# One large and one small output store, moved from ScalarE's DMA queue to the end of SyncE's, in an 8192 x 8192 adjacency product

## The chip, the cores and the metric

The kernel runs on one core of a Trainium2 chip. The time is the device time of one execution in microseconds (us). Three executions were timed; the median is 645.89 us. One more was profiled.

## The reference

```
keep   = (u >= 0.1)                       # u: 8192 x 64
x_drop = x * keep / 0.9                   # x: 8192 x 64
y      = x + matmul(adj, x_drop)          # adj: 8192 x 8192, fp32, 268 MB
out    = (y - mean(y)) / sqrt(var(y) + 1e-5)   # over the 64 columns
```

All operands are fp32. adj is read once and each element is used for one product with 64 columns, so the traffic is almost wholly the reading of adj.

## The kernel before

Partition p holds the 64 rows 64p to 64p + 63 of x, u and the output. "A row" below is one such index, 0 to 63, taken on all 128 partitions, so one row of the output is 128 x 64 numbers, 256 bytes in each partition. The host has laid adj out in blocks, so that every load is 128 long contiguous runs.

The work goes over rows. Rows 0 to 59 are done in 12 groups of 5 (a loop). For each group, 64 tiles of adj (128 x 640 each) come in three loads (24, 24 and 16 tiles) into `adj_ring`, which has room for one whole group. TensorE multiplies the transposed way: `x_drop` is the stationary operand, adj the moving one, and even and odd tiles go to the upper and the lower half of PSUM. VectorE copies the sum to SBUF, TensorE turns it back with `twofold`, and `normalise` on VectorE with a square root on ScalarE (line 178) writes the result over x in SBUF; it ends with an increment of `normed_ready`.

After the loop come two groups with smaller loads, the tail: rows 60 to 62 together (five pieces of 26, 15, 11, 8 and 4 tiles, each tile 128 x 384, into `tail_acc0`), and row 63 alone (nine pieces of 13, 16, 12, 8, 6, 4, 2, 2 and 1 tiles, each 128 x 128). The last three tiles of row 63 are multiplied the direct way into `final` (line 235), so that the last step needs no turning back.

Order of the loads: all loads of adj are issued by SyncE (SP), on its DMA queue, in the order in which TensorE uses them. Each waits on `adj_used` until the part of the ring that it writes over is free; for the tail these are waits on the last three chunks of the loop, so that the last piece has no wait later than the loop's end (line 160). When SP's queue can take no more, the instruction that issues a load takes long.

Order of the stores: ScalarE issues three on its own queue. The first (line 186) holds rows 0 to 59, 1920 KB, and waits for `normed_ready` = 12; the second (line 191) holds rows 60 to 62, 96 KB, and waits for 13; the third (line 196) is row 63, 32 KB. ScalarE's last instruction waits for all three (line 197). The area that the stores read is not written again.

Of the kernel before, what the change touches and what calls it, by code (L numbers as in the profile page):

```python
# [6 lines left out]
D = 64  # L7
P = 128
KT = N // P
# [6 lines left out]
R = 5  # L16
FULL = 12
# [12 lines left out]
LAST = len(TAIL) - 1  # L30
# [24 lines left out]
def build(nc: bass.Bass, xu: bass.AP, adj: bass.AP, out: bass.AP):  # L55
# [6 lines left out]
    out_rows = out.rearrange("(p t) d -> p (t d)", p=P)  # L62
# [6 lines left out]
    def tail_block(start, width):  # L69
        first = (FULL * RING + start) * P  # L70
        return adj[first:first + width * P].rearrange("(p c) -> p c", p=P)

    with ExitStack() as ctx:
# [3 lines left out]
        def sem(name):  # L77
            return ctx.enter_context(nc.semaphore(name))

        def ps(name, cols):  # L80
# [9 lines left out]
        normed = x_nat  # L90
# [22 lines left out]
        chunk_loaded = [sem(f"chunk_loaded{s}") for s in range(SLOTS)]  # L113
        piece_loaded = [[sem(f"piece_loaded{n}_{i}") for i in range(len(tiles))]
                        for n, (_, tiles) in enumerate(TAIL)]

        adj_used = sem("adj_used")
# [2 lines left out]
        zeros_ready = sem("zeros_ready")  # L120
        identity_ready = sem("identity_ready")
        twofold_ready = sem("twofold_ready")
        halved_ready = sem("halved_ready")
        acc_copied = sem("acc_copied")
        back_ready = sem("back_ready")
        sum_ready = sem("sum_ready")
# [8 lines left out]
        normed_ready = sem("normed_ready")  # L135
        final_stats = sem("final_stats")
        final_var = sem("final_var")
        out_stored = sem("out_stored")
# [3 lines left out]
        @block.sync  # L142
        def _(sp):
            def load(s, group):
                first, width = SLOT_FIRST[s] * TILE, SLOT_TILES[s] * TILE
                sp.dma_start(adj_ring[:, first:first + width], slot_block(s)[group]).then_inc(chunk_loaded[s], 16)  # L146

            sp.dma_start(x_and_u[:], xu).then_inc(x_loaded, 16)  # L148
            for s in range(SLOTS):
                load(s, 0)  # L150
            with sp.Fori(1, FULL) as group:
                for s in range(SLOTS):

                    sp.wait_ge(adj_used, (group - 1) * SLOTS + s + 1)
                    load(s, group)
            for n in range(len(TAIL)):
                for i, (_, _, at, width) in enumerate(pieces(n)):

                    slot = sum(at + width > first * TILE for first in SLOT_FIRST)
                    sp.wait_ge(adj_used, MAIN - SLOTS + slot)  # L160
                    sp.dma_start(adj_ring[:, at:at + width], tail_block(at, width)).then_inc(piece_loaded[n][i], 16)  # L161

        @block.gpsimd
        def _(pool):
            nc.gpsimd.memset(eps[:], EPS).then_inc(eps_ready, 1)  # L165
            nc.gpsimd.memset(identity[:], 0.0).then_inc(zeros_ready, 1)
            pool.wait_ge(zeros_ready, 1)
            nc.gpsimd.affine_select(out=identity[:], in_=identity[:], compare_op=ALU.not_equal, fill=1.0,
                                    base=0, pattern=[[-1, P]], channel_multiplier=1).then_inc(identity_ready, 1)

            pool.wait_ge(identity_ready, 1)
            nc.gpsimd.tensor_tensor(twofold[:], identity[:, 0:D], identity[:, D:P], ALU.add).then_inc(twofold_ready, 1)

        @block.scalar
        def _(act):
            def root(n, rows):
                act.wait_ge(squares_ready, n + 1)
                nc.scalar.activation(std[:, 0:rows], squares[:, 0:rows], ACT.Sqrt, scale=1.0 / D,  # L178
                                     bias=eps[:]).then_inc(std_ready, 1)

            act.wait_ge(eps_ready, 1)
            with act.Fori(0, FULL) as g:
                root(g, R)
            act.wait_ge(normed_ready, FULL)
            cols = slice(0, FULL * R * D)
            act.dma_start(out_rows[:, cols], normed[:, cols]).then_inc(out_stored, 16)
            for n in range(LAST):
                root(FULL + n, TAIL[n][0])
            act.wait_ge(normed_ready, FULL + LAST)
            cols = slice(FULL * R * D, (KT - 1) * D)  # L190
            act.dma_start(out_rows[:, cols], normed[:, cols]).then_inc(out_stored, 16)
            act.wait_ge(final_var, 1)
            nc.scalar.activation(std[:, 0:1], mean_var[:, 1:2], ACT.Sqrt, bias=eps[:]).then_inc(std_ready, 1)  # L193
            act.wait_ge(normed_ready, FULL + LAST + 1)
            cols = slice((KT - 1) * D, KT * D)
            act.dma_start(out_rows[:, cols], normed[:, cols]).then_inc(out_stored, 16)
            act.wait_ge(out_stored, 16 * 3)

        @block.tensor
        def _(pe):  # L200
# [26 lines left out]
            for n, (rows, _) in enumerate(TAIL):  # L227
                for i, (before, count, at, _) in enumerate(pieces(n)):
                    pe.wait_ge(piece_loaded[n][i], 16)
                    for t in range(before, before + count):  # L230
                        col = at + (t - before) * rows * P
                        if n < LAST or t < HALVED:
                            last = product(tail_acc[n], rows * P, col, t, KT if n < LAST else HALVED)
                        else:
                            last = nc.tensor.matmul(final[:, 0:D], adj_ring[:, col:col + P],  # L235
                                                    x_drop[:, t * D:(t + 1) * D], start=False, stop=(t == KT - 1))
                    last.then_inc(adj_used, 1)
                    if n == LAST and i == 0:

                        turn_back(TAIL[n - 1][0], FULL + n - 1)  # L240
                        nc.tensor.matmul(final[:, 0:D], identity[:], x_nat[:, (KT - 1) * D:KT * D],  # L241
                                         start=True, stop=False)
                    if n == LAST and i == len(TAIL[n][1]) - 2:

                        pe.wait_ge(acc_copied, FULL + LAST + 1)
                        nc.tensor.matmul(final[:, 0:D], acc_sb[:, 0:P], twofold[:], start=False, stop=False)  # L246
# [104 lines left out]
```

## Time and profile before

| | |
|---|---|
| median of 3 runs | 645.89 us (645.62 to 645.92) |
| profiled execution | 645.73 us |
| its span in the profile | 643.8 us |
| outside the span | 1.93 us |
| HBM read, written | 272.63 MB, 2.10 MB |
| PE busy, DVE busy, ACT busy | 512.4, 60.8, 19.6 us |

Every time in the rows is in us from the span's start, unless marked ns. PE is TensorE's matmul, PEld its weight load, DVE is VectorE, ACT is ScalarE; SPq and ACTq are the DMA-issuing instructions of SyncE and ScalarE. q1 is the DMA queue of SyncE, q10 that of ScalarE (its bytes are those of the three stores). An fp32 matmul shows as two instructions in a count.

### The profile page before, as it was taken

What the parts mean: (1) busy time and instruction counts of PE and PEld (TensorE: products, weight loads), DVE (VectorE), ACT (ScalarE), POOL (GpSimd) and SP (SyncE); (2) the same over time, 40 slices, a digit from 0 to 9 for tenths busy, and PEclk for the clock granted to TensorE, in tenths of its full rate; (3) what the DMA queues carried; (4) which work ended last, traced back from release to release, by engine and by line L of the source; (5) the groups of instructions that cost most, each with busy time, mean ns of one, the idle gap of its engine ahead of it and who ended that gap; (6) DMA issues with size and microseconds to landing.
All of it is one profiled execution on the core that took longest, in us unless ns stands there. A gap on an engine that the chain in (4) does not pass through costs nothing.

```text
span 643.8 us, 7619 instructions
## 1 busy us (share of the span) xinstructions
PE 512.4 (80%) x3458; PEld 265.4 (41%) x3458; DVE 60.8 (9%) x268; ACT 19.6 (3%) x26; POOL 1.1 (0%) x8
## 2 busy tenths in 40 slices
PE   0088798698798698798698798798798887888987
PEld 0044344344344344444344444444443443444436
DVE  1200200200200200100200200200200110110202
ACT  0000000000000000000000000000000000000000
POOL 0000000000000000000000000000000000000000
PEclk9997988988988987989878988988987987979999
DMA  9999999999999999999999999999999999999996
GB/s 383 428 429 444 432 428 440 428 435 440 428 431 444 428 428 448 428 428 448 428 428 448 428 428 448 428 428 448 428 428 448 428 428 448 428 428 408 421 427 253
DMA packets 7780, 274.80 MB, mean 427 GB/s; under 512 B 992, under 2 KB 1504, under 8 KB 2272
## 3 DMA queue, kind: packets, MB, share of 16 engines
q1 hardware_dynamic: 7344, 272.63, 98.2%
q10 hardware_dynamic: 432, 2.10, 0.8%
q8 instruction: 4, 0.07, 0.0%
HBM read 272.63 MB, written 2.10 MB: 427 GB/s over the span
## 4 chain that ended last, share of the span: by engine, by line
DMA 69%; PE 30%; SPq 0%; issue 0%; DVE 0%; ACT 0%
DMA adj_ring<-adj_blocks 69%; PE acc L203 28%; PE tail_acc L203 2%; SPq L146 0%; PE final L235 0%; PE back L210 0%; SPq L161 0%; SPq L148 0%; DVE x_and_u L316 0%; PE final L246 0%; ACT std L193 0%; DVE stats L310 0%; PE final L241 0%; DVE mean_var L312 0%; DVE rstd L314 0%
## 5 line engine op out<-in xcount | busy, mean ns | idle before, releaser
L203 PE MATMUL acc<-adj_ring,x_and_u 128*64 128x320 f32 x3072 | 465.4, 468 | 114.1 <-DMA adj_ring<-adj_blocks 114.1
L203 PEld LDWEIGHTS acc<-adj_ring,x_and_u 128*64 128x64 f32 x3072 | 233.2, 149 | 341.0 <-DMA adj_ring<-adj_blocks 122.3
L253 DVE COPY acc_sb<-acc 128x320 f32<-128x320 f32 x24 | 10.7, 486 | 517.4 <-PE acc L203 517.4
L203 PE MATMUL tail_acc<-adj_ring,x_and_u 128*64 128x384 f32 (+1 forms) x250 | 29.0, 384 | 2.2 <-DMA adj_ring<-adj_blocks 2.1
L210 PE MATMUL back<-twofold,acc_sb 128*128 128x64 f32 x126 | 16.8, 280 | 11.9 <-DVE acc_sb L253 11.9
L210 PEld LDWEIGHTS back<-twofold,acc_sb 128*128 128x128 f32 x126 | 15.0, 191 | 18.8 <-DVE acc_sb L253 18.7
L178 ACT ACTIVATE std<-squares,eps 128x5 f32<-128x5 f32 (+1 forms) x13 | 3.9, 300 | 615.1 <-DVE squares L278 615.1
L203 PEld LDWEIGHTS tail_acc<-adj_ring,x_and_u 128*64 128x64 f32 x250 | 15.9, 137 | 14.9 <-issue 10.8
L178 ACT ACT_TABLE_LOAD x12 | 15.4, 1283 | 1.2 <-POOL eps L165 1.0
L284 DVE TENSOR_SCALAR x_and_u<-summed,mean,rstd 128x64 f32 (+1 forms) x63 | 15.2, 309 | 0.5
L262 DVE BATCH_NORM_STATS2 stats<-summed 128x6 f32<-128x64 f32 x63 | 9.3, 213 | 0.4
L258 DVE TENSOR_TENSOR summed<-back,x_and_u 128x320 f32<-128x320 f32 (+1 forms) x13 | 6.3, 482 | 20.3 <-PE back L210 20.3
L293 DVE SCALAR_TENSOR_TENSOR x_and_u<-x_and_u 128x1024 f32<-128x1024 f32 x4 | 4.9, 1220 | 12.9 <-DMA x_and_u<-xu 12.9
L253 DVE COPY acc_sb<-tail_acc 128x384 f32<-128x384 f32 (+1 forms) x2 | 0.9, 426 | 23.1 <-PE tail_acc L203 23.1
L281 DVE RECIPROCAL rstd<-std 128x5 f32<-128x5 f32 (+1 forms) x13 | 2.5, 190 | 4.8 <-ACT std L178 4.8
L297 DVE TENSOR_SCALAR x_and_u<-x_and_u 128x1024 f32<-128x1024 f32 x4 | 2.8, 693 | 0.1
L276 DVE TENSOR_SCALAR mean<-twice_mean 128x5 f32<-128x5 f32 (+1 forms) x13 | 2.2, 172 | 0.0
L268 DVE TENSOR_TENSOR gap<-stats 128x5 f32<-128x5 f32 (+1 forms) x13 | 2.2, 169 | 0.5
L269 DVE TENSOR_TENSOR within<-stats 128x5 f32<-128x5 f32 (+1 forms) x13 | 2.1, 160 | 0.0
L270 DVE TENSOR_TENSOR twice_mean<-stats 128x5 f32<-128x5 f32 (+1 forms) x13 | 2.1, 160 | 0.0
L278 DVE TENSOR_TENSOR squares<-within,between 128x5 f32<-128x5 f32 (+1 forms) x13 | 2.1, 160 | 0.0
L272 DVE SCALAR_TENSOR_TENSOR between<-gap 128x5 f32<-128x5 f32 (+1 forms) x13 | 2.0, 157 | 0.0
(19 smaller groups left out, 5.8 us busy)
## 6 DMA issues: line engine op xcount, KB each, us to landing
adj_ring<-adj_blocks SPq DMA_DIRECT2D x24, 7680.0 KB, 33.3
adj_ring<-adj_blocks SPq DMA_DIRECT2D x12, 5120.0 KB, 36.9
adj_ring<-adj_blocks SPq DMA_DIRECT2D x1, 4992.0 KB, 26.0
x_and_u<-xu SPq DMA_DIRECT2D x1, 4096.0 KB, 12.1
adj_ring<-adj_blocks SPq DMA_DIRECT2D x1, 2880.0 KB, 17.6
adj_ring<-adj_blocks SPq DMA_DIRECT2D x1, 2112.0 KB, 26.2
out<-x_and_u ACTq DMA_DIRECT2D x1, 1920.0 KB, 13.8
adj_ring<-adj_blocks SPq DMA_DIRECT2D x1, 1536.0 KB, 29.9
```

The lines of the kernel that those rows point to most:

```text
L178: nc.scalar.activation(std[:, 0:rows], squares[:, 0:rows], ACT.Sqrt, scale=1.0 / D, bias=eps[:]).then_inc(std_ready, 1)
L203: return nc.tensor.matmul(into[h * D:(h + 1) * D, 0:cols], x_drop[:, t * D:(t + 1) * D], adj_ring[:, at:at + cols], start=(t < 2), stop=(t ...
L210: last = nc.tensor.matmul(back[:, r * D:(r + 1) * D], acc_sb[:, r * P:(r + 1) * P], twofold[:], start=True, stop=True)
L253: last = nc.vector.tensor_copy(acc_sb[:, b * cols:(b + 1) * cols], part[:, 0:cols])
L258: nc.vector.tensor_tensor(summed[:, 0:rows * D], back[:, 0:rows * D], x_nat[:, bass.ds(row * D, rows * D)], ALU.add).then_inc(sum_ready, 1)
L262: last = nc.vector.bn_stats(stats[:, r, :], summed[:, r * D:(r + 1) * D])
L268: nc.vector.tensor_tensor(gap[:, 0:rows], m0, m1, ALU.subtract).then_inc(gap_ready, 1)
L276: nc.vector.tensor_scalar(mean[:, 0:rows], twice_mean[:, 0:rows], 0.5, None, ALU.mult)
L281: nc.vector.reciprocal(rstd[:, 0:rows], std[:, 0:rows]).then_inc(rstd_ready, 1)
L284: last = nc.vector.tensor_scalar(normed[:, bass.ds((row + r) * D, D)], summed[:, r * D:(r + 1) * D], mean[:, r:r + 1], rstd[:, r:r + 1], A ...
L293: nc.vector.scalar_tensor_tensor(out=x_drop[:, cols], in0=x_drop[:, cols], scalar=P_DROP, in1=x_nat[:, cols], op0=ALU.is_ge, op1=ALU.mult) ...
L297: nc.vector.tensor_scalar(x_drop[:, cols], x_drop[:, cols], 1.0 / (1.0 - P_DROP), None, ALU.mult).then_inc(drop_ready, 1)
```

## The change

The waits and the stores of rows 0 to 59 and 60 to 62 are taken off ScalarE and put at the end of SyncE's program, behind the issue of the last piece of adj. The third store stays on ScalarE. The semaphore `halved_ready`, which nothing used, is dropped.

```diff
@@ @block.sync
                     sp.wait_ge(adj_used, MAIN - SLOTS + slot)
                     sp.dma_start(adj_ring[:, at:at + width], tail_block(at, width)).then_inc(piece_loaded[n][i], 16)
 
+            sp.wait_ge(normed_ready, FULL)
+            cols = slice(0, FULL * R * D)
+            sp.dma_start(out_rows[:, cols], normed[:, cols]).then_inc(out_stored, 16)
+            sp.wait_ge(normed_ready, FULL + LAST)
+            cols = slice(FULL * R * D, (KT - 1) * D)
+            sp.dma_start(out_rows[:, cols], normed[:, cols]).then_inc(out_stored, 16)
+
@@ @block.scalar
             with act.Fori(0, FULL) as g:
                 root(g, R)
-            act.wait_ge(normed_ready, FULL)
-            cols = slice(0, FULL * R * D)
-            act.dma_start(out_rows[:, cols], normed[:, cols]).then_inc(out_stored, 16)
             for n in range(LAST):
                 root(FULL + n, TAIL[n][0])
-            act.wait_ge(normed_ready, FULL + LAST)
-            cols = slice(FULL * R * D, (KT - 1) * D)
-            act.dma_start(out_rows[:, cols], normed[:, cols]).then_inc(out_stored, 16)
             act.wait_ge(final_var, 1)
```

On ScalarE, behind the loop, the program before reads (128x3840 is the store of rows 0 to 59, 128x192 that of rows 60 to 62, 128x64 that of row 63; `std` is the square root):

```order
L182 COMPARE_AND_BRANCH
L186 DMA out<-x_and_u 128x3840
L178 ACTIVATE std<-squares,eps 128x3
L191 DMA out<-x_and_u 128x192
L193 ACTIVATE std<-mean_var,eps 128x1
L196 DMA out<-x_and_u 128x64
```

and now, with the line numbers of the changed file:

```order
L188 COMPARE_AND_BRANCH
L184 ACTIVATE std<-squares,eps 128x3
L193 ACTIVATE std<-mean_var,eps 128x1
L196 DMA out<-x_and_u 128x64
```

Two stores and their waits are gone from ScalarE; its two square roots and the last store are in the same order. At the end of SyncE's program, where the last small pieces of adj are issued, it was:

```order
L161 DMA adj_ring<-adj_blocks 128x512
L161 DMA adj_ring<-adj_blocks 128x256 x2
L161 DMA adj_ring<-adj_blocks 128x128
L73 UNCONDITIONAL_BRANCH
```

and is now:

```order
L160 DMA adj_ring<-adj_blocks 128x512
L160 DMA adj_ring<-adj_blocks 128x256 x2
L160 DMA adj_ring<-adj_blocks 128x128
L164 DMA out<-x_and_u 128x3840
L167 DMA out<-x_and_u 128x192
L73 UNCONDITIONAL_BRANCH
```

Both stores stand behind all fourteen pieces of the tail. TensorE, VectorE and GpSimd run the same instructions in the same order.

## Rows read from the trace of the kernel before

**Rows 1.** The page: span, queues (packets, MB, share of 16 engines), chain, costliest wait.
```profile
span 643.8 us, 7619 instructions
q1 hardware_dynamic: 7344, 272.63, 98.2%
q10 hardware_dynamic: 432, 2.10, 0.8%
DMA 69%; PE 30%; SPq 0%; issue 0%; DVE 0%; ACT 0%
L203 PE MATMUL acc<-adj_ring,x_and_u 128*64 128x320 f32 x3072 | 465.4, 468 | 114.1 <-DMA adj_ring<-adj_blocks 114.1
```

**Rows 2.** The chain of work that ended last, from 597: start, length, what.
```profile
597.31 29.93 DMA adj_ring<-adj_blocks
...
627.28 5.67 PE tail_acc L203 x50
632.95 0.81 PE back L210 x6
...
633.99 5.39 PE tail_acc L203 x96
639.38 0.59 PE final L235 x4
...
641.55 0.34 DVE x_and_u L316
```

**Rows 3.** Timeline of TensorE, the tail: start, length, instructions, [idle before <-releaser].
```profile
607.27 13.76 PE L203 MATMUL tail_acc<-adj_ring,x_and_u 128*64 128x384 f32 x82
607.65 0.14 PEld L203 LDWEIGHTS tail_acc<-adj_ring,x_and_u 128*64 128x64 f32 x2 [0.18 <-issue]
...
619.90 0.14 PEld L203 LDWEIGHTS tail_acc<-adj_ring,x_and_u 128*64 128x64 f32 x1 [0.18 <-issue]
...
623.08 0.20 PEld L203 LDWEIGHTS tail_acc<-adj_ring,x_and_u 128*64 128x64 f32 x4 [2.72 <-DMA adj_ring<-adj_blocks]
...
627.28 0.20 PEld L203 LDWEIGHTS tail_acc<-adj_ring,x_and_u 128*64 128x64 f32 x4 [0.78 <-DMA adj_ring<-adj_blocks]
...
631.21 1.50 PEld L203 LDWEIGHTS tail_acc<-adj_ring,x_and_u 128*64 128x64 f32 x26 [0.50 <-DMA adj_ring<-adj_blocks]
...
639.30 0.52 PEld L235 LDWEIGHTS final<-x_and_u,adj_ring 128*128 128x128 f32 x4 [0.17 <-DMA adj_ring<-adj_blocks]
```

**Rows 4.** Timeline of ScalarE's DMA issues, the three stores.
```profile
611.22 0.38 ACTq L186 DMA_DIRECT2D out<-x_and_u  x1
...
636.65 0.34 ACTq L191 DMA_DIRECT2D out<-x_and_u  x1
...
641.93 0.34 ACTq L196 DMA_DIRECT2D out<-x_and_u  x1
```

**Rows 5.** DMA issues: KB, us from issue to landing.
```profile
adj_ring<-adj_blocks SPq DMA_DIRECT2D x1, 2112.0 KB, 26.2
out<-x_and_u ACTq DMA_DIRECT2D x1, 1920.0 KB, 13.8
adj_ring<-adj_blocks SPq DMA_DIRECT2D x1, 1536.0 KB, 29.9
out<-x_and_u ACTq DMA_DIRECT2D x1, 96.0 KB, 2.9
adj_ring<-adj_blocks SPq DMA_DIRECT2D x1, 64.0 KB, 13.7
out<-x_and_u ACTq DMA_DIRECT2D x1, 32.0 KB, 1.5
```

**Rows 6.** SyncE's issues of the 2112 KB and the last two pieces.
```profile
596.83 0.43 SPq L161 DMA_DIRECT2D adj_ring<-adj_blocks  x1
```
```profile
611.48 14.08 SPq L161 DMA_DIRECT2D adj_ring<-adj_blocks  x1
```
```profile
625.61 1.68 SPq L161 DMA_DIRECT2D adj_ring<-adj_blocks  x1
```

**Rows 7.** DMA queues from 614 to 623: packets, MB, share of 16 engines.
```profile
q10 hardware_dynamic: 127, 1.95, 50.9%
q1 hardware_dynamic: 141, 1.86, 48.4%
```

**Rows 8.** DMA engines' busy tenths from 637.2 to 639.3, in 40 slices.
```profile
DMA  4231244998882211212232322313312111100000
```

**Rows 9.** The same with GB/s, 641.9 to 643.8: the last store.
```profile
DMA  0000000000000000002697400000000000000000
GB/s 0 0 0 0 0 0 0 0 0 0 0 0 0 0 0 0 0 0 65 146 232 157 76 16 0 0 0 0 0 0 0 0 0 0 0 0 0 0 0 0
```

**Rows 10.** Stretch, length, busy PE, PEld, DVE, ACT, POOL; granted clock, DMA share, GB/s.
```profile
607.30:639.30 32.00, 29.83 (x259) 16.80 (x258) 6.12 (x33) 0.60 (x2) 0.00 (x0) 1.00 0.96 398
```

More of the change, by code:

```diff
@@ L122, in build @@
         twofold_ready = sem("twofold_ready")
-        halved_ready = sem("halved_ready")
         acc_copied = sem("acc_copied")
```

## The prediction, made before the changed kernel ran

> **What bounds the kernel now.** I read the page first: its queues, its chain and its costliest wait [rows 1]. The loads of adj keep the 16 DMA engines busy for 98.2% of the span, TensorE waits 114.1 us for them in the loop, and the chain is 69% DMA. So the loop goes at the pace of the loads, and the change touches nothing in it: the first moved store was issued at 611.22 [rows 4], behind the loop. The question is the last 33 us.
>
> Next the chain from 597 on [rows 2]. It is DMA until 627.24, and then TensorE to 640.5 with no further DMA in it, then a short run of VectorE and ScalarE that ends at 641.89 (641.55 + 0.34). So two things end nearly together: the reader should see that TensorE, not the loads, has the last 12 us, but that its start at 627.28 was set by a load.
>
> Then TensorE's timeline in the tail [rows 3]. A tile of rows 60 to 62 takes 0.322 us: the weight loads go from 607.65 to 619.90 in 38 steps, (619.90 - 607.65) / 38 = 0.3224. The 64 tiles of this group would take 64 x 0.3224 = 20.63 us with all data there, 607.27 to 627.90. The next group's first weights are loaded at 631.21. TensorE has thus lost 631.21 - 627.90 = 3.31 us to late pieces. The three waits in the rows say the same: 2.72 + 0.78 + 0.50, less the usual 0.18 before any weight load three times, is 3.46. A fourth, before the last direct tiles at 639.30, is 0.17.
>
> Last the DMA queues in the same stretch [rows 7]. From 614 to 623, just when TensorE waits longest, the large store takes 50.9% of the engines' time and the loads 48.4%. The loads are late because the store goes between them.
>
> **The change part by part.**
>
> The store of rows 0 to 59 leaves the stretch of the loads. It is 1920 KB = 1.966 MB. Its rate in engine time was 1.95 MB / (0.509 x 9.0 us) = 426 GB/s, that of the loads 1.86 / (0.484 x 9.0) = 427 [rows 7]. So it costs the loads 1.966 / 0.426 = 4.6 us. The piece of 2112 KB landed at 596.83 + 26.2 = 623.03 [rows 5, 6]; by then 1.95 MB of the store were gone, so it will land near 618.5. TensorE comes to it at 607.27 + 41 x 0.3224 = 620.49: 2.0 us to spare. The piece of 1536 KB landed at 597.31 (its issue begins the DMA part of the chain [rows 2]) + 29.9 = 627.2 [rows 5] and will land near 622.6; TensorE needs it 11 tiles later, at 624.0: 1.4 us to spare. The piece behind the third wait arrived at 631.2, when TensorE went on [rows 3], and will at about 626.6; its use moves to 627.9: 1.3 us to spare. Behind it the loads are moved by 4.6 us and TensorE by 3.3, so every later piece is safe by the margin it has now and 1.3 us more; the last landed at 625.61 + 13.7 = 639.3 [rows 5, 6] and will at about 634.7, or 634.4 with the next point.
>
> The store of rows 60 to 62, 96 KB, also went between the last loads (issued 636.65, landed 2.9 later [rows 4, 5]). Its packets are part of the thin stretch from 637.2 to 639.1 [rows 8], in which a few engines only are still at work. I put its removal at 0.3 us for the last loads, between 0 and 0.5; nothing on TensorE hangs on it once the margin is there.
>
> Gain on the path: 3.31 us of waits, and perhaps the 0.17 at 639.30, between 3.3 and 3.6 us. The clock gives nothing more: it is granted in full (2.4 GHz, 1.00) through this stretch already [rows 10]. TensorE's last product then ends at about 637.2 instead of 640.5, and the last store, which follows it after the unchanged VectorE and ScalarE steps, is issued at 641.93 - 3.3 = 638.6. That is the sum, if the moved stores have no part in the end.
>
> Cost of the new place. SyncE's issue: two instructions of 0.4 us on an engine that has nothing behind them. Their order behind the last piece matters: SyncE was held up when its queue was full, 14.08 us for the last but one piece and 1.68 for the last [rows 6], the latter until 627.29, just when the 1536 KB landed. With earlier landings the last piece is accepted at about 622.7, and the large store one landing later, near 624.5. It has to be in the queue by 634.4, so it is, by 10 us, and no load waits behind it. The wait for `normed_ready` = 12 has then been met for 13 us; that for 13 (met at about 633.3) holds only the 96 KB store.
>
> The DMA engines. What they have to move before the last store is the same set of bytes as before, and they do not idle. Before, the last of them was done at about 639.1 (the last busy slice is number 37 of 40 slices of 0.0525 us from 637.2 [rows 8]). If a store packet costs an engine the same at the end as in the middle, then the engines that are late with their loads are done with loads and stores again at about 639.1; the others earlier. The last store is issued at 638.6, and its first packet comes 0.85 us after its issue (the first busy slice is 18 of 40 in 641.9 to 643.8, so 642.75 [rows 9]), that is at 639.45. It finds the engines free by 0.3 us. It lands 1.5 us after issue [rows 5], at 640.1. A store by SyncE that ends at 639.1 needs about 0.4 us from its last packet to its landing (for the last store: last busy slice to 643.04, landing at 643.43 [rows 4, 5, 9]), so 639.5, and would have to be 0.6 us later before it ends the kernel.
>
> What this rests on is the rate of a store that runs alone, on all 16 engines at once; the trace shows none of size. Bounds: 426 GB/s from the engine time above, which costs nothing; and 1.95 MB in 9.0 us = 217 GB/s, the most that was in fact written at one time [rows 7]. At 217 the store takes 9.06 us, 4.46 more, less the 0.6 to spare: 3.9 us lost, which turns the gain of 3.3 into a loss of 0.6. I take 426, since the row is one of packets of the same size and engines, and since reads at 427 beside it show that an engine's packet and not HBM sets the pace; the other end stays in the range's reasoning.
>
> The Trainium skill, DMA: Bandwidth & Descriptors, Where 436 GB/s comes from, says that for transfers between HBM and SBUF the HBM side binds at about 358 GB/s for a core. This trace has a mean of 427 for loads and does not agree; by the page the store would take 5.5 us, 0.9 more, and the gain would be 3.0.
>
> Sum: the profiled execution took 645.73 us, 643.8 of span and 1.93 around it. 645.73 - 3.3 = 642.4. That execution stands 0.16 below the median of the runs (645.89); taking 3.4 off the median gives 642.5. I say 642.4.
>
> **The rivals.**
>
> A, no change. All bytes pass the same 16 engines, whichever queue holds them; if the end were theirs, order would be nothing. For it: the engines are busy for 0.96 of the time from 607.3 to 639.3 [rows 10]. Against: after 639.1 they idle [rows 8, 9] until 642.75 while TensorE and VectorE finish; that hole is where the store goes. It would also come out so if the engines let the loads gain nothing, or if stores alone ran at about 230 GB/s: 1.966 / 0.23 = 8.5 us, 3.9 more than 4.6. Time 645.7.
> The Trainium skill, DMA: Bandwidth & Descriptors, Issuing engines are not separate DMA queues, says that DMAs of all issuing engines run on the same 16 DMA engines and interleave, so that issuing from several saves only issue time. By that rule, taken alone, the move would be worth nothing, 645.7. The trace agrees that they share (50.9% and 48.4%), but TensorE's waits show that the order among them counts.
>
> B, partly covered. The stores run alone at some 300 GB/s (6.55 us, 1.95 more, 0.6 of it free), or the last store meets their end and takes 2.9 us to land, as the 96 KB store did beside loads, instead of 1.5. Either costs 1.35 to 1.4: gain 1.9, time 643.8. For it: the 0.3 and 0.6 us of room are thin. Against: the equal cost of a packet in both directions.
>
> C, slower: the stores end the kernel. Place: from the last load's landing at 634.4 on, all engines write to HBM at once. The only stretch of pure writing in the trace is the last store, whose three fullest slices are at 146, 232 and 157 GB/s, 178 in the mean [rows 9]. At 178 the large store takes 11.0 us, 6.4 more, 5.8 after the room: the gain of 3.3 becomes a loss of 2.5, time 648.2. It is a loss from 231 GB/s down, and one that shows from about 200 down. Against: that store has packets of 256 bytes, where the moved one has 15 KB, and the large store wrote at 217 with half the engines' time.
>
> **How the numbers follow.** Forecast 0.72, B 0.14, A with its near neighbours 0.09, C 0.05. This kernel's measurement can tell about 0.2% (1.3 us) from no change. The forecast and nearly all of B are faster by more: 0.86. A, and the end at 217 GB/s (646.3): 0.09. Slower 0.05. The forecast's own range is 641.9 to 643.0; with B it reaches to 644.5; below, 641.8 if the waits were worth 3.6 and a run is 0.3 off.
>
> **What would show it.** In the profile after: TensorE's matmuls of `tail_acc` from 607 to about 633 with no wait for DMA; the 2112 KB piece landing near 618.5 and the last piece near 634.5; q10 with 32 KB only; the large store's packets between about 632 and 639 at over 400 GB/s; the last issue on ScalarE near 638.6 and its landing 1.5 us later, the latest of the three. The prediction is wrong if waits for DMA remain in the tail (the loads gained nothing), if the large store lands after 640.1, or if DMA engines idle between the last load and the large store (it was issued late).

## The result and the profile after

The changed kernel takes 644.12 us in the median of 6 runs, against 645.80 before (6 runs): ratio 0.9973, 95% interval 0.9963 to 0.9983. It is faster by 1.7 us, where 3.3 to 3.4 were forecast. The six runs are not one cluster: 642.38 and 642.52, 644.05 and 644.20, 645.38 and 645.58. Those before lie within 645.62 to 646.00. So the forecast time is met by two runs of six, and the rest are 1.7 or 3.1 us above it. The profiled execution is one of the middle pair (644.20, span 642.4).

The first lines of its page (queue: packets, MB, share of 16 engines):

```profile
span 642.4 us, 7619 instructions
...
q1 hardware_dynamic: 7632, 274.70, 99.2%
...
q10 hardware_dynamic: 144, 0.03, 0.0%
...
DMA 65%; PE 34%; DVE 0%; issue 0%; SPq 0%; ACT 0%
```

The two stores are in SyncE's queue, and the DMA part of the chain has become shorter [rows 1]. The chain of the changed kernel from 550 on (start, length, what):

```profile
549.97 33.36 DMA adj_ring<-adj_blocks
583.34 0.04 issue
583.38 23.47 PE acc L203 x160
606.85 0.02 issue
606.87 0.90 DVE acc_sb L253 x2
...
607.82 1.33 PE back L210 x10
609.14 22.31 PE tail_acc L203 x154
...
632.49 5.39 PE tail_acc L203 x96
637.88 0.59 PE final L235 x4
...
640.06 0.34 DVE x_and_u L316
```

The reader should see that the last DMA in the chain ends at 583.34, where before it ended at 627.24 [rows 2]: TensorE now sets the time for the last 57 us. In the tail its timeline reads:

```profile
609.07 22.38 PE L203 MATMUL tail_acc<-adj_ring,x_and_u 128*64 128x384 f32 x154
...
629.77 1.45 PEld L203 LDWEIGHTS tail_acc<-adj_ring,x_and_u 128*64 128x64 f32 x24 [0.18 <-issue]
...
637.81 0.52 PEld L235 LDWEIGHTS final<-x_and_u,adj_ring 128*128 128x128 f32 x4 [0.17 <-issue]
```

One unbroken run of 154 instructions now stands where 82 [rows 3] and 72 stood with a wait between them, and no wait names a DMA. The 72, in the kernel before:

```profile
623.09 9.86 PE L203 MATMUL tail_acc<-adj_ring,x_and_u 128*64 128x384 f32 x72 [2.06 <-DMA adj_ring<-adj_blocks]
```

From the first product of the tail to the last direct ones it takes 637.81 - 609.07 = 28.74 us instead of 639.30 - 607.27 = 32.03 [rows 3]: 3.29 us less, where 3.31 were forecast. But the tail begins at 609.07 instead of 607.27, 1.80 us later, and 3.29 - 1.80 = 1.49 is what the profiled execution gained (645.73 - 644.20 = 1.53).

Where the 1.80 us come from is seen in TensorE's granted clock behind its last wait in the loop, for the second chunk of the last group. The same stretch, first before, then after (stretch, length, busy PE, PEld, DVE, ACT, POOL, granted clock, DMA share, GB/s):

```profile
583.40:586.80 3.40, 3.40 (x26) 1.79 (x27) 0.00 (x0) 0.00 (x0) 0.00 (x0) 1.00 0.89 386
```
```profile
583.40:586.80 3.40, 3.40 (x14) 1.64 (x16) 0.00 (x0) 0.00 (x0) 0.00 (x0) 0.53 0.89 386
```

26 products against 14 in the same 3.4 us: after the wait the clock was granted at its lower level, 1.2 GHz, in the changed kernel, and in full in the kernel before. 3.4 us at half speed put TensorE back by 1.7; the other 0.1 is the load of the chunk, which landed at 583.34 instead of 583.22. TensorE's wait for it was not alike (before, then after; the weight loads show it):

```profile
583.26 21.19 PEld L203 LDWEIGHTS acc<-adj_ring,x_and_u 128*64 128x64 f32 x160 [2.67 <-DMA adj_ring<-adj_blocks]
```
```profile
583.38 0.20 PEld L203 LDWEIGHTS acc<-adj_ring,x_and_u 128*64 128x64 f32 x4 [3.26 <-DMA adj_ring<-adj_blocks]
```

It idled 0.6 us longer in the changed kernel, before any store is issued; the last section comes back to this.

The stores, by their issues on SyncE and ScalarE, and by KB and us to landing:

```profile
622.92 1.97 SPq L164 DMA_DIRECT2D out<-x_and_u  x1
...
635.15 0.34 SPq L167 DMA_DIRECT2D out<-x_and_u  x1
...
640.43 0.37 ACTq L196 DMA_DIRECT2D out<-x_and_u  x1
```
```profile
out<-x_and_u SPq DMA_DIRECT2D x1, 1920.0 KB, 15.1
...
out<-x_and_u SPq DMA_DIRECT2D x1, 96.0 KB, 4.5
adj_ring<-adj_blocks SPq DMA_DIRECT2D x1, 64.0 KB, 13.7
out<-x_and_u ACTq DMA_DIRECT2D x1, 32.0 KB, 1.5
```

The large store landed at 622.92 + 15.1 = 638.0, the small at 639.65, both ahead of the last store (641.9). The last piece of adj landed at 621.21 + 13.7 = 634.9 (forecast 634.4 to 634.7), so in the next two microseconds the engines wrote the stores and loaded nothing more of adj (DMA share and GB/s last):

```profile
635.00:636.00 1.00, 1.00 (x24) 1.00 (x22) 0.12 (x1) 0.00 (x0) 0.00 (x0) 1.00 1.08 461
636.00:637.00 1.00, 1.00 (x24) 1.00 (x21) 0.00 (x0) 0.00 (x0) 0.00 (x0) 1.00 1.01 430
```

Per engine time, worked out as the prediction did from [rows 7], these are 461 / 1.08 = 427 and 430 / 1.01 = 426 GB/s, the same rate as there.

### The profile page after: what moved, and what is told of

It reads as the page before. It is cut to its first block, busy times and chain, and to the rows that moved or that the text cites. A ratio compares the mean times of both kernels' runs of the same rounds, so it can differ in the third digit from the quotient of the medians.

```text
span 642.4 us, 7619 instructions
## 1 busy us (share of the span) xinstructions
PE 508.3 (79%) x3458; PEld 264.1 (41%) x3458; DVE 60.7 (9%) x268; ACT 19.6 (3%) x26; POOL 1.1 (0%) x8
## 4 chain that ended last, share of the span: by engine, by line
DMA 65%; PE 34%; DVE 0%; issue 0%; SPq 0%; ACT 0%
DMA adj_ring<-adj_blocks 65%; PE acc L203 29%; PE tail_acc L203 4%; PE back L210 0%; SPq L145 0%; DVE acc_sb L253 0%; PE final L235 0%; SPq L147 0%; DVE x_and_u L316 0%; PE final L246 0%; ACT std L193 0%; DVE stats L310 0%; PE final L241 0%; DVE mean_var L312 0%; DVE rstd L314 0%
## 6 DMA issues: line engine op xcount, KB each, us to landing
adj_ring<-adj_blocks SPq DMA_DIRECT2D x1, 2112.0 KB, 20.6
out<-x_and_u SPq DMA_DIRECT2D x1, 1920.0 KB, 15.1
```

## The experiments

Theory 1: the change gives its 3.3 us in the tail in every run; what varies is how long TensorE runs at 1.2 GHz behind its wait near 583, which nothing absorbs any more. Rival: the stores at the end cost time, and their landing varies.

**The changed kernel again.** The kernel is the same; only the runs are new.

> The changed kernel once more, unchanged, for its spread. Theory 1 (clock): the six runs of the changed kernel lie in three pairs, 642.4, 644.1 and 645.5, because the granted clock after TensorE's wait of about 3 us for the second chunk of the last loop group (near 583) is 1.2 GHz for 0, 3.4 or about 6.8 us; nothing behind it waits for a DMA any more, so each microsecond at half clock costs half a microsecond at the end. The runs here should fall near the same three values, and the profile should have one of them: a span of 640.5 if 583 to 590 is granted 1.00, 642.3 if about 0.76, 643.6 if about 0.5. Rival 2 (stores): the spread comes from the large store at the end, which lands late in some runs; then in a slow profile the last landing is that of SyncE's store, and TensorE's last product ends near 637.3 in all. Expected median between 642.4 and 645.5.

Measured: 642.31, 642.39, 643.95, 643.98, 644.06, 644.10; median 643.96, ratio 0.9968 (0.9956 to 0.9980). This time the profiled execution is one of the lowest pair, 642.39, span 640.6. Its stretch and its tail:

```profile
583.40:586.80 3.40, 3.40 (x26) 1.79 (x27) 0.00 (x0) 0.00 (x0) 0.00 (x0) 1.00 0.89 386
```
```profile
607.27 22.38 PE L203 MATMUL tail_acc<-adj_ring,x_and_u 128*64 128x384 f32 x154
```

With the clock granted in full, the tail starts at 607.27, as before, runs through in the same 22.38 us, and the execution takes 642.39. TensorE's wait at 583 was 2.67 us here, as in the kernel before. Over both sets, 4 of 12 runs of the changed kernel are at 642.3 to 642.5, 6 at 644.0 to 644.2 and 2 at 645.4 to 645.6.

**Unread products ahead of the loop's waits.**

```diff
+WARM = (32, 24, 0)
...
                 for s in range(SLOTS):
+                    for i in range(WARM[s]):
+                        h = i % 2
+                        nc.tensor.matmul(final[h * D:(h + 1) * D, 0:P], twofold[:], identity[:], start=True, stop=True)
                     pe.wait_ge(chunk_loaded[s], (g + 1) * 16)
```

> The changed kernel with products nobody reads (32 and 24 of 128 columns, into a bank not yet in use) before the waits for the first and the second chunk of each loop group, so that TensorE idles there about 1 to 1.5 us instead of 3 to 5. Theory 1 (clock): the clock stays at 2.4 GHz, the spread goes, all runs at 642.2 to 642.6. Rival 2 (stores set the spread): no difference, median near 644.1 with values up to 645.5. Rival 3 (the added products delay TensorE or the loads): slower than the changed kernel, 645 or more.

Measured: 642.30, 642.37, 642.47, 642.51 and one run at 644.11; median 642.47, ratio 0.9956 (0.9942 to 0.9969). Mean granted clock 0.963 in the profile, 0.906 without the products. The wait before 583 was still long, which is what the expectation had wrong (it said 1 to 1.5 us):

```profile
565.03 12.58 PEld L204 LDWEIGHTS acc<-adj_ring,x_and_u 128*64 128x64 f32 x96 [1.18 <-DMA adj_ring<-adj_blocks]
583.17 21.19 PEld L204 LDWEIGHTS acc<-adj_ring,x_and_u 128*64 128x64 f32 x160 [2.63 <-DMA adj_ring<-adj_blocks]
```

With the clock up behind 565, TensorE was through with the first chunk sooner, and so waited 2.63 us in spite of the 24 products.

**More of them.** `WARM = (40, 44, 0)`, else as above.

> The changed kernel with more unread products: 40 before the first chunk's wait and 44 before the second's, so that TensorE idles only about 0.4 us before the chunk at 583 instead of 2.6. Theory 1 (clock): the one run at 644.1 with fewer products came from a fall of the clock behind that 2.6 us wait; now all runs are at 642.2 to 642.6. Rival: the one run at 644.1 had another cause, and some runs still show it. Rival: the added products end after the chunk has landed and delay TensorE: up to 643.

The wait at 583 as forecast:

```profile
583.49 21.19 PEld L204 LDWEIGHTS acc<-adj_ring,x_and_u 128*64 128x64 f32 x160 [0.44 <-DMA adj_ring<-adj_blocks]
```

Measured: 642.41 to 642.70 in all five runs, median 642.51, ratio 0.9950 (0.9937 to 0.9964). The spread is gone, and this is the lowest ratio of all, 3.2 us under the kernel before (645.70 beside it), though its interval overlaps that of the version with fewer products.

**The same products in the kernel before.** The edit of `WARM = (32, 24, 0)` on the kernel before.

> The kernel before with the same unread products. Theory 1: in it TensorE waits again for DMA in the tail until 627.3, so whatever the clock did at 583 is absorbed there; with the clock kept up the time stays at 645.6 to 646.0. Rival: if the unread products gain something by themselves (for instance by releasing ring space and so loads earlier), this kernel gains as well, 643 to 645.

Measured: eight of eleven runs at 645.69 to 645.85, three at 646.55 to 646.63; median 645.81, ratio 1.0003 (0.9994 to 1.0012). So the products gain nothing by themselves; they only gain where the tail has no wait left. The profile is of one of the three at 646.6 (646.55) and shows the same mechanism at another place; the other two have no profile. Behind its tail wait of 2.71 us, at 622.9, the clock was at half:

```profile
622.91 0.20 PEld L204 LDWEIGHTS tail_acc<-adj_ring,x_and_u 128*64 128x64 f32 x4 [2.71 <-DMA adj_ring<-adj_blocks]
```
```profile
623.80:627.00 3.20, 3.20 (x14) 1.22 (x12) 0.00 (x0) 0.00 (x0) 0.00 (x0) 0.51 1.00 415
```

These 3.2 us at half clock cost TensorE 1.6. The next wait, 0.78 in [rows 3] and absent here, gave back 0.6 of it (all but the usual 0.18), and the time is 0.8 above the median of the kernel before.

**Without the large store.** The three lines of `sp.wait_ge(normed_ready, FULL)` and the store of rows 0 to 59 are taken out of the changed kernel, so these rows are not written.

> The changed kernel with the store of rows 0 to 59 left out (these rows of the output are not written). Theory: at the end of SyncE's queue the store is wholly hidden behind TensorE's last products, so leaving it out changes nothing: the same three values 642.4, 644.1, 645.5, and a median within 0.3% of that of the changed kernel. Rival (partly covered): if the store at the end costs something, this kernel is faster in its fastest runs, 641.5 or less.

Measured: 642.32, five runs at 643.87 to 644.13, 645.00; median 644.10, ratio 0.9972 (0.9961 to 0.9983). The same as with the store: the large store is wholly hidden, and it has no part in the spread.

**Both stores late, but on ScalarE's queue.** In the kernel before:

```diff
+            for n in range(LAST):
+                root(FULL + n, TAIL[n][0])
+            act.wait_ge(piece_loaded[LAST][len(TAIL[LAST][1]) - 1], 16)
             act.wait_ge(normed_ready, FULL)
             cols = slice(0, FULL * R * D)
             act.dma_start(out_rows[:, cols], normed[:, cols]).then_inc(out_stored, 16)
-            for n in range(LAST):
-                root(FULL + n, TAIL[n][0])
             act.wait_ge(normed_ready, FULL + LAST)
```

> The kernel before, with both stores still issued by ScalarE on its own queue, but only when the last piece of adj has landed (a wait on that piece's semaphore ahead of them). Theory (order, not queue): what counts is that the stores come behind the loads; the waits of the tail go as in the changed kernel, 642.4 to 644.1 by the clock. The stores start about 1 us after the last landing instead of at once, so they end near 640.3; that may add up to 0.5 us. Rival (the queue itself matters, for instance because SyncE's queue is filled further): times near 645.7. Rival (the stores' cover is thin): a late start of 1 us shows fully, fastest runs 643.4.

Measured: 643.54, 643.58, 643.96, 644.00, 644.85, 645.24, 645.39; median 644.00, ratio 0.9977 (0.9966 to 0.9988). The median is that of the changed kernel, and TensorE has no wait for a load in the tail (the 154 instructions below are one run): for the loads it is the order that counts, not the queue. But the fastest runs are 1.2 us above those of the changed kernel, near what the second rival said: the store is issued at 635.0, when the last piece has landed, and lands at 635.0 + 6.2 = 641.2, where the last store of a run at full clock lands at 638.6 + 1.5 = 640.1. In SyncE's queue it landed at 638.0. So 3.2 us of delay cost about 1.2, and the cover of the large store in the changed kernel is about 2 us. (The small store lands late here too, at 636.3 + 6.3 = 642.6 in the profiled execution; no profile of one of the fastest runs shows which of the two ends it.) The profiled execution, 645.24, is one of the upper three. It is the only profile of a kernel with the stores late that is more than 2 us above 642.4, and shows what the third cluster most likely is; no run of the changed kernel itself near 645.5 was profiled:

```profile
583.40:589.50 6.10, 6.10 (x26) 2.77 (x28) 0.00 (x0) 0.00 (x0) 0.00 (x0) 0.53 1.00 430
```
```profile
610.17 22.38 PE L204 MATMUL tail_acc<-adj_ring,x_and_u 128*64 128x384 f32 x154
```

The mean clock is 0.53 over 6.1 us instead of 3.4, and the tail starts at 610.17, 2.9 us late.

**The large store alone, the small store alone.** One of the two is moved, the other stays on ScalarE.

> The changed kernel with the 96 KB store back on ScalarE's queue; only the large store is behind the loads. Theory: the large store alone made the loads late, so the whole gain stays: 642.3 in the fastest runs, 644.0 in the next ones. Rival: if the small store held the last pieces up by its 0.3 us where it counts, the fastest runs are at 642.6 or more.

> The kernel before with only the 96 KB store moved behind the loads. Theory: TensorE's last 12 us have no wait for a load but one of 0.17 us, so nothing to win: 645.5 to 645.8. Rival: the last pieces are what counts, gain of 0.3 us or more, 645.4 or less.

Measured: the large store alone 642.33, 642.36, 643.94, 644.08, 644.14 (median 643.94, ratio 0.9961, 0.9947 to 0.9975), all of the gain, and its fastest runs are those of the changed kernel; the small one alone 645.53 to 645.97 in eleven runs (median 645.67, ratio 0.9999, 0.9990 to 1.0008), nothing, as the two expectations said.

## Why the prediction was right or wrong

*The large store made the loads late, and its move ends TensorE's waits in the tail, 3.31 us.* Right: 3.29 measured, all of it from the large store. The piece of 2112 KB landed at 598.64 + 20.6 = 619.2 (predicted 618.5), 3 us ahead of its use in that execution, and at 596.83 + 22.2 = 619.0 in the one at full clock, 1.5 us ahead (predicted 2.0). The two small terms beside it were worth nothing: the 0.17 before the last direct tiles is still there with no load to wait for (637.81 above), and the small store alone, put at 0.3 for the last loads, gains nothing in the time.

*The moved stores have no part in the end.* Right: leaving the large one out changes nothing, and pure writing went at the 426 GB/s per engine time that the prediction took; the bound of 217 and the 178 of rival C are far off. I gave 0.6 us of room to the landing of a store by SyncE, at 639.5. At full clock the small one landed at 633.35 + 6.3 = 639.65, 0.5 us before the last store, but the large one at 638.0, 2.1 us before it: for the large store the room was put too small. Its issue was taken at 622.92 + 1.97 = 624.9 (forecast 624.5).

*The sum, 645.73 - 3.3.* Here it failed, in its silent term, put at nothing: that TensorE starts the tail at 607.27 in every execution, as before. I wrote that "the clock gives nothing more: it is granted in full (2.4 GHz, 1.00) through this stretch already", and looked at the tail alone. The wait of 2.67 us at 583 has full clock behind it in the profile of before, but the waits at 565 (3.64 us, last section) and 534 (4.05 us) have half clock behind them in the same trace. Which level TensorE gets behind such a wait differs from one execution to the next. Before the change, 1.7 or 2.9 us lost at 583 would only make TensorE reach the late pieces of the tail later: even 2.9 us late it needs the 1536 KB piece at 624.0 + 2.9 = 626.9, and that landed at 627.2. So the waits that the change took out were also a buffer that could hide this. That they did hide it is inferred: all 41 timed runs of the kernel before lie within 645.5 to 646.0, and the unread products gain nothing in it, but all three profiles of kernels that keep the large store early have full clock at 583, so none shows a loss being absorbed there; the profile at 646.55 shows a partial one in the tail. The term that was missing is 0 in a third of the runs, about 1.7 us in half of them and about 3 in the rest: 1.6 at the median, which is 642.4 against 644.0 (median of the 12 runs).

*The rivals.* Median and B (643.8) are near each other by number only; its causes are refuted, a cover that is partly missing by the store left out, and a last store slowed to 2.9 us by its landing in 1.5. A is refuted by TensorE's waits, which did go; the two runs near 645.5 are near its time by number only. C did not come.

*The range*, 641.8 to 644.5, held the median, and ten of twelve single runs. That is luck: the forecast's own range was 641.9 to 643.0, which held four of the twelve and not the median, and it reached to 644.5 only for B, whose cause did not come.

## What to carry to other kernels

When a change takes out the last wait that an engine had for data, ask what that wait was absorbing. Follow the engine back to the previous wait, compare the granted clock behind several such waits in the trace, and price the spread as a term of its own. If it decides, work that nobody reads can keep TensorE from idling there; here it turned 644.0 with a spread of 3 us into 642.5 with one of 0.3. Here the large store, ready early, belonged behind the loads, since the compute of the last pieces outlasted it; in the loads' own queue it started as they ended, and on the other queue, held until the last landing, it cost 1.2 us in the fastest runs.

## What the runs showed that was not expected

Behind one and the same wait, that at 583, TensorE's clock was at half for about 3.4 us of work, for about 5.6 us or not at all, and the times of the changed kernel lie in three clusters. The trace of the kernel before has the longer stretch behind its wait at 565 (stretches of 1 us; granted clock third from the end):

```profile
563.00:564.00 1.00, 0.00 (x0) 0.00 (x0) 0.62 (x7) 0.30 (x1) 0.00 (x0) 1.00 0.14 61
564.00:565.00 1.00, 0.00 (x0) 0.00 (x0) 0.94 (x5) 0.99 (x1) 0.00 (x0) 0.60 0.57 246
570.00:571.00 1.00, 1.00 (x6) 0.44 (x4) 0.00 (x0) 0.00 (x0) 0.00 (x0) 0.50 0.00 0
571.00:572.00 1.00, 1.00 (x10) 0.56 (x8) 0.00 (x0) 0.00 (x0) 0.00 (x0) 0.99 1.85 799
```

It began while TensorE still waited and went on for about 6 us of work. What decides between the three is not settled by these runs, but the difference between the executions is there before 583, where none of the kernels without unread products differs from another yet. The clock came back behind the wait at 565 at 571.0 in three profiles (before, the changed kernel again, the small store alone), and TensorE then waited 2.65 to 2.67 us at 583; it came back at 570.0, 569.4 and 568.6 in the profiled changed kernel, the one without the large store and the one with both stores late on ScalarE's queue. There TensorE was through with its chunk sooner, and the wait was 3.26, 3.56 and 3.88 us. The wait at 583 was 2.62 to 2.67 us in five profiles (before, the changed kernel again, the unread products in both kernels, the small store alone), all with full clock behind it; 2.81 us (the large store alone, where the clock fell 1.1 us after TensorE went on) and the three longer ones had half clock. But the length of a wait is not the whole of it: one unprofiled run of five with the 24 unread products took 644.11, and in the tail a wait of 2.71 us had half clock behind it in one trace, and one of 2.72 [rows 3] full clock in another. Only with the wait cut to 0.44 us did all the runs of a version, five, stay together.
